# Weight products and averages moved to banks without other users, loads behind the first slot, the last two images drained apart (four-layer attention and mixer, one core)

## What is computed

```python
x = attention(x, L0)   # q, k of 16 channels, v of 128; gamma * softmax(q k^T) v + x
x = mixer(x, L1)       # 2-D Hartley transform, two block-diagonal layers with relu, shrink, back, + x
x = attention(x, L2)   # as layer 0
x = gn_attention(x, L3)  # group norm (32 groups), q, k, v of 128, softmax(q k^T / sqrt(128)) v wo + bo, + x
```

## Time and profile before

| what | us |
|---|---|
| median of the timed runs | 118.61 |
| the profiled execution, its own time | 117.25 |
| its span | 115.5 |
| PE busy | 102.2 (89%) |
| DVE, ACT, POOL busy | 69.5, 64.9, 56.3 |
| granted TensorE clock, mean | 0.992 |

### The profile page before, as it was taken

How to read it: one execution, slowest core, us unless ns; L and a number is a source line. 1 busy time by engine, 2 the same in 40 slices (tenths; PEclk the granted TensorE clock), 3 DMA queues, 4 the chain that set the end, 5 groups by cost and what they waited for, 6 DMA issues and landing times.

```text
span 115.5 us, 2858 instructions
## 1 busy us (share of the span) xinstructions
PE 102.2 (89%) x1004; PEld 86.9 (75%) x1004; DVE 69.5 (60%) x278; ACT 64.9 (56%) x186; POOL 56.3 (49%) x109
## 2 busy tenths in 40 slices
PE   5688799989997799999998699995999999999670
PEld 5267698989875688888887588974989797998540
DVE  0126567695977267777461869687586765466511
ACT  5028385756554166663647686755756554777520
POOL 0100390000576538888403364669987979844400
PEclk9999999999999999999999999999999999999996
DMA  2999400000000000000000000000000011101121
GB/s 83 215 271 414 178 0 0 6 3 0 3 6 0 0 0 0 6 0 0 0 6 0 3 9 0 0 0 0 6 0 0 0 45 45 48 25 49 48 68 45
DMA packets 3182, 4.57 MB, mean 40 GB/s; under 512 B 480, under 2 KB 2400, under 8 KB 3168
## 3 DMA queue, kind: packets, MB, share of 16 engines
q1 hardware_dynamic: 2160, 2.61, 7.3%
q10 hardware_dynamic: 1008, 1.78, 4.5%
HBM read 3.34 MB, written 1.05 MB: 38 GB/s over the span
## 4 chain that ended last, share of the span: by engine, by line
PE 74%; DMA 6%; ACT 6%; DVE 5%; POOL 3%; issue 3%; SPq 1%; DVEq 0%
PE banks L703 11%; PE banks L677 8%; PE banks L697 7%; PE banks L602 6%; PE banks L638 6%; DMA xt_in<-in_x_t 6%; PE banks L755 4%; PE banks L628 4%; PE banks L772 4%; PE banks L586 4%; PE banks L654 3%; PE banks L613 3%; PE banks L796 3%; ACT probs_t L893 3%; PE banks L734 2%
## 5 line engine op out<-in xcount | busy, mean ns | idle before, releaser
L504 POOL TENSOR_SCALAR hidden<-first,ident_columns 64x260 f32<-64x260 f32 x16 | 19.6, 1228 | 19.0 <-DVE first L1116 18.3
L885 ACT ACTIVATE probs<-negated,lowest 128x256 f32<-128x256 f32 x48 | 23.9, 500 | 7.5 <-DVE negated L1035 6.4
L452 POOL TENSOR_TENSOR probs<-probs,inverse 128x256 f32<-128x256 f32 x32 | 19.1, 612 | 15.8 <-DVE inverse L1049 15.4
L893 ACT ACTIVATE probs_t<-banks 128x512 f32<-128x512 f32 x24 | 14.3, 595 | 12.8 <-PE banks L677 12.7
L703 PE MATMUL banks<-probs_t,v 128*128 128x256 f32 x64 | 17.6, 397 | 1.6 <-ACT probs_t L893 1.6
L677 PE MATMUL banks<-ident_columns,probs 128*128 128x128 f32 x96 | 14.8, 275 | 1.4 <-issue 1.0
L1035 DVE TENSOR_SCALAR_CACHE_REDUCE negated<-banks 128x256 f32<-128x256 f32 x32 | 12.2, 416 | 2.7 <-PE banks L654 2.7
L703 PEld LDWEIGHTS banks<-probs_t,v 128*128 128x128 f32 x64 | 11.1, 190 | 3.5 <-ACT probs_t L893 2.3
L677 PEld LDWEIGHTS banks<-ident_columns,probs 128*128 128x128 f32 x96 | 11.1, 141 | 3.1 <-issue 1.5
L1049 DVE RECIPROCAL inverse<-total 128x1 f32<-128x1 f32 x48 | 7.2, 158 | 9.5 <-ACT probs L885 8.0
L1041 DVE TENSOR_SCALAR_CACHE_REDUCE negated<-banks,v 128x256 f32<-128x256 f32 x16 | 7.1, 480 | 5.1 <-PE banks L638 4.9
(11 more groups left out here) (109 smaller groups left out, 198.7 us busy)
## 6 DMA issues: line engine op xcount, KB each, us to landing
out<-stream SPq DMA_DIRECT2D x7, 128.0 KB, 1.9
rows<-in_x_rows ACTq DMA_DIRECT2D x1, 768.0 KB, 10.4
xt_in<-in_x_t SPq DMA_DIRECT2D x1, 512.0 KB, 8.5
constants<-in_constants SPq DMA_DIRECT2D x1, 450.0 KB, 10.1
layer<-in_layer ACTq DMA_DIRECT2D x1, 256.5 KB, 8.6
xt_in<-in_x_t SPq DMA_DIRECT2D x2, 128.0 KB, 4.1
rows<-in_x_rows ACTq DMA_DIRECT2D x1, 256.0 KB, 4.9
xt_in<-in_x_t SPq DMA_DIRECT2D x1, 256.0 KB, 6.8
```

Source lines behind the costliest of these rows:

```text
L452: pool.tensor_tensor(probs[:, half(job), tile, :], probs[:, half(job), tile, :], inverse[:, at, tile:tile + 1].to_broadcast([TILE, TOKENS] ...
L504: pool.tensor_scalar(halves(hidden[HC:C, half(job), side]), strided(first[own, half(job)], SUMS, -SUMS, SUMS), column["b1n"][own], 0.0, AL ...
L885: nc.scalar.activation(probs[:, half(job), tile, :], negated[:, half(job), tile, :], ACT.Exp, bias=lowest[:, half(job), tile:tile + 1], sc ...
L893: nc.scalar.activation(flat(probs_t[:, half(job)]), probs_t_bank, ACT.Copy).then_inc(probs_t_ready, 1)
```

## The change

No matmul is added or taken away. What moves:

- **Banks.** Weight products go to bank 2 (`prepared_strip`), two in a slot: mixer0 and mixer1 in slot 5, mixer2 and mixer3 in slot 7, weights3 and values3 in slot 19, bias3 in slot 21. `project_pair` and the first `forward_tokens` wait (`strip_taken`) until DVE has taken them. Averages go to banks 3 and 6 (means) and 2 and 7 (variances), each with the waits that this needs. The mixer's second product uses banks 0 and 1 in turn, g of image 0 bank 7. Bank 5 is left to the turned probabilities, which no longer wait for any of these.
- **Order.** In the slots of PE the energies of a pair come ahead of `forward_tokens`, and in slots 10 and 11 the second product ahead of `mix_values`. POOL normalizes first in its slot. 
- **Loads.** ACT issues x in rows and values after its part of slot 0, layer3 after slot 3.
- **End.** One drain slot is left for ACT and POOL, none for PE and DVE. The energies of the last image are made in its own slot. The last image but one gets its own banks and its probabilities are copied by DVE; the last one is scaled by DVE, and turned, copied, mixed, added and stored in two halves.

PE, slot 19: before, first product of the new layer's second pair to the next mix.

The diff, cut to its core:

```diff
-DRAIN = 3
+SLOTS = len(JOBS) + 1
+LAST = JOBS[-1]
...
-PREPARED = {3: "weights3", 4: "values3", 5: "mixer0", 6: "mixer1", 7: "mixer2", 8: "mixer3",
-            9: "bias3"}
+PREPARED = {5: ["mixer0", "mixer1"], 7: ["mixer2", "mixer3"], 19: ["weights3", "values3"],
+            21: ["bias3"]}
...
+        def prepared_strip(k):
+            return banks[:, 2, k * TOKENS:k * TOKENS + C + 3]
+        def mean_bank(pair):
+            return banks[:, 3 if pair < 2 else 6, 0:PAIR]
+        def variance_bank(pair):
+            return banks[:, 2 if pair == 0 else 7, 0:PAIR]
+        def g_bank(job):
+            return banks[:, 7 if job.image == 0 else 4, 0:TOKENS]
+        def y_bank(job):
+            return banks[:, half(job), 0:TOKENS]
...
+                if ahead is not None and ahead.layer == NORMED:
+                    normalize(ahead)
                 if spread_pair is not None:
                     channel_spreads(spread_pair)
                 if scale_pair is not None:
                     norm_scales(scale_pair)
-                if ahead is not None and ahead.layer == NORMED:
-                    normalize(ahead)
-                if scales(weighed):
+                if scales(weighed) and weighed != LAST:
                     scale_probs(weighed)
...
+            def project_pair(job, now):
+                if prepared_until(now):
+                    pe.wait_ge(strip_taken, prepared_until(now))
...
-                if job == Job(MIXER + 1, 0):
-                    pe.wait_ge(y_ready, BATCH)
-                elif job == Job(0, BATCH - 1):
-                    pe.wait_ge(y_ready, 1)
-                elif nth(job) > 1:
+                if nth(job) > 1:
                     pe.wait_ge(probs_t_ready, nth(job) - 1)
-                if sides_until(now):
-                    pe.wait_ge(side_taken, sides_until(now))
...
+            def transpose_last(tile):
+                if tile > 0:
+                    pe.wait_ge(probs_t_ready, nth(LAST) - 2)
+                pe.wait_ge(last_scaled, tile + 1)
...
+            def mix_last(tile):
+                pe.wait_ge(last_turned_ready, tile + 1)
...
                 if i == 0:
                     pe.wait_ge(mixer_ready, 6)
-                    pe.wait_ge(probs_t_ready, BATCH - 1)
-                    pe.wait_ge(side_taken, len(PREPARED))
+                if i < 2:
+                    pe.wait_ge(negated_ready, BATCH * TILES)
                 else:
-                    pe.wait_ge(probs_t_ready, BATCH)
-                    pe.wait_ge(y_ready, i)
+                    pe.wait_ge(y_ready, i - 1)
...
                 if i < 2:
                     pe.wait_ge(negated_ready, BATCH * TILES)
+                    pe.wait_ge(g_ready, 1)
...
             def group_variances(pair):
                 pe.wait_ge(spread_ready, pair + 1)
+                if pair == 0:
+                    pe.wait_ge(u_ready, 2 * BATCH)
+                else:
+                    pe.wait_ge(negated_ready, 2 * BATCH * TILES)
+                    pe.wait_ge(group_var_ready, pair)
...
-                if sides_until(now) > sides_until(now - 1) and by_age(now - 1, 3, 2):
-                    pe.wait_ge(probs_t_ready, nth(by_age(now - 1, 3, 2)))
...
+                    pe.wait_ge(u_ready, nth(this))
+                    for k, name in enumerate(PREPARED[now]):
+                        prepare(name, k)
+                if mixes(back2) and by_age(now, 4, 3):
+                    second_product(back2)
                 if by_age(now, 4, 3):
                     mix_values(by_age(now, 4, 3))
                 if mixes(back3):
                     backward_channels(back3)
-                if mixes(back2):
+                if mixes(back2) and not by_age(now, 4, 3):
                     second_product(back2)
...
+                if this == LAST:
+                    energies(this)
...
+            transpose_next_to_last()
+            mix_values(JOBS[-3])
+            mix_next_to_last()
+            for tile in range(TILES):
+                transpose_last(tile)
+            for tile in range(TILES):
+                mix_last(tile)
...
-            load_x(act, 0)
-            act.dma_start(values[:, :], values_d).then_inc(values_loaded, 16)
-            act.dma_start(layer3[:, :], layer3_d).then_inc(layer3_loaded, 16)
-            load_x(act, 1)
...
+                if now == 0:
+                    load_x(act, 0)
+                    act.dma_start(values[:, :], values_d).then_inc(values_loaded, 16)
+                    load_x(act, 1)
+                if now == 3:
+                    act.dma_start(layer3[:, :], layer3_d).then_inc(layer3_loaded, 16)
...
+            copy_next_to_last()
+            for tile in range(TILES):
+                invert_total(LAST, tile)
+                scale_last(tile)
+            add_residual(JOBS[-3])
+            add_next_to_last_residual()
+            for tile in range(TILES):
+                add_last_residual(tile)
```

More of the change, by code:

```diff
@@ L172, with prepared_until @@
            "gamma0", "gamma2", "bq0", "bk0", "bq2", "bk2"]
-def sides_until(slot):
-    made = [now for now in PREPARED]
-    for pair in range(BATCH // PAIR):
-        last = (NORMED - 1) * BATCH + pair * PAIR + PAIR - 1
-        made += [last + MEANS_AT, last + MEANS_AT + 1]
-    return sum(now <= slot for now in made)
+def prepared_until(slot):
+    return sum(len(names) for now, names in PREPARED.items() if now <= slot)
 def build(nc, x_rows_d, x_t_d, ident_columns_d, constants_d, plain_d, values0_d, values_d,
```

171 lines of the change are left out of this document (121 added, 50 removed).

## The result

| | before | after |
|---|---|---|
| median of the runs beside each other | 118.53 us (6 runs) | 109.97 us (6 runs) |
| their range | 117.37 to 119.95 | 109.82 to 110.37, one 113.76 |
| profiled execution, own time | 117.25 | 110.37 |
| its span | 115.5 | 108.6 |

The ratio is 0.931, 95% interval 0.926 to 0.936. The forecast was 112.1 us, the range 110.4 to 115.4: the time lies 0.4 us under its low end. Ratios leave out executions that lie more than 1.5% over the fastest of their kernel; medians here are over all of them.

The account below looks back on a forecast made before the run. PE, busy 102.2 of 115.5 us, was taken to bound the kernel, leaving gaps between its matmuls to shorten. Terms summed to -6.5: 110.75 profiled, 112.1 us with the timed runs' 1.36 offset; range 110.4 to 115.4.

Parts of the forecast that it names:

- step E: Slots 24 and 25: first normalized image sooner, but group_variances waits for spreads and a negation; -0.2 us, bias3 counted apart.
- A: Start to the first mix: weight products and waits gone, x sooner, less ACT's issues; -2.1 us.
- The 1.05 for ACT's issues: At the start: ACT's load issues delay its exponents and next copy, a cost of 1.05 us, between 0 and 2.36.
- The 0.7 for earlier x: At the start: the first two pieces of x land sooner with fewer loads beside them, a gain of 0.7 us.
- B: Slots 4 to 7: PE's wait in slot 7 for DVE to empty bank 5 goes, with its restart; -0.6 us.
- C: Slots 8 to 11, hand-over from layer 0 to the mixer: idle and restarts of 3.36 us fall to 1.2; -2.2 us.
- D: Slots 19 and 20: weights3 and values3 return, project_pair waits for DVE's takes; +0.6 us, between 0 and 1.25.
- F: Layer 3: projections no longer wait for POOL, about 0.43 us instead of 0.70; -0.5 us.
- G: The end: last image finished in halves, 2.8 us instead of 4.4 from exponents to residual; -1.5 us, between -0.7 and -2.
- Rival 1: At the start: the loads don't land sooner, constants still at 14.25; 114.0 us, chance 0.17.
- Rival 2: The removed waits come back elsewhere as DVE and ACT chains decide; 115.2 us, chance 0.18.
- Rival 3: ACT is held by its own load issues, so every exponent waits; slower, 120.3 us, chance 0.03.

Follow-up runs that it names:

- e11: Changed kernel with its four later loads issued by SyncE instead of ScalarE, behind the same events: 109.65 us.
- e10: Changed kernel with the mixer's second product back in bank 5 and its third back in bank 4: 112.88 us.
- e8: Changed kernel with projection ahead of energies in slot 18 and prepared products taken before the values are moved in slot 19: 109.48 us, ratio 0.923.
- e4: Changed kernel with the end as before (three draining slots, general code for the last images): 111.51 us.
- e1: The kernel before, unchanged, timed again: 118.79 us, ratio 1.001.
- e13: Changed kernel with one warm-up product instead of three: 111.3 us.
- e6: Kernel before with the later loads moved behind the first slot and five warm-up products instead of three: 117.35 us, ratio 0.992.
- e2: Kernel before with only the loads of x in rows, values and layer3 moved behind the first slot: 119.99 us.
- e12: Kernel before with five warm-up products instead of three, loads all up front: 118.25 us, ratio 1.001.
- e5: Kernel before with four warm-up products instead of three, loads all up front: 117.94 us.
- e9: The changed kernel, unchanged, timed again: 110.07 us, ratio 0.927.
- e14: Changed kernel with the two orders of e8 and the SyncE loads of e11 together: median 111.53 us, best 108.53.
- e15: e14 with four warm-up products instead of three: 109.25 us, ratio 0.919.
- e7: Changed kernel with four warm-up products instead of three: 110.32 us.

## Why the prediction was nearly right, and where it failed

**The mechanism and the sum.** Against its own profiled execution the forecast was 110.75 us; measured 110.37. Only step E has the wrong sign, by 0.4 us.

- **A** gained 2.57, not 2.1, and for other reasons. The 1.05 for ACT's issues was nothing (e11, and what the exponents waited for): a time of issue on ACT's queue was added to a chain that hangs on VectorE. I had the idle 1.32 us in hand and subtracted it as if the issues came behind each other with the moves; they run beside the moves. By the Trainium skill ("DMA: Bandwidth & Descriptors", section "Issuing engines are not separate DMA queues") initiating is usually small relative to the DMA; the rows of 0.33 to 0.59 us, two beside the moves and one inside the wait, agree beside 4.7 to 6.2 us to landing, and the total by that rule, 111.1, was nearer. The 0.7 for earlier x did not come either: the pieces landed 0.5 us sooner, and the first projection ran at half speed and took 0.86 us more, so that the values start where they did (6.64 and 6.67). That a cost of 1.05 us which did not come and a gain of 0.7 which did not come partly cancel is luck. The constants landed at 9.2, so POOL's diagonals were ready at 12.3, and mixer0 was asked for at 15.26: covered, as forecast.
- **B and C** were forecast as -3.3 with bias3 and came as -2.95. B was -0.7 for -0.6; C was -1.7 for -2.2. The waits that C left were named: in slot 9 the copy holds the mix for 0.24 us, the second product of image 0 waits 0.29. What was mis-sized is the restart. Its 0.28 us is the difference between a mix of 1.17 and one of 0.89. But a mix right behind the second product takes 1.09 without any wait:

```profile
33.03 0.59 PE banks L829 x8
33.62 1.09 PE banks L726 x8
```

  Two such mixes stand in this stretch, so about 0.4 us (an estimate from these rows) of the restarts' price stayed. e10 shows that the banks are what removed the rest.
- **D** +1.12 for +0.6. The wait for the strip was foreseen (0.61 here); the 0.37 us and restart of layer 2's first energies behind y of the last image were not. The diff puts `y_ready` in front of them, since y now lies in the banks of the energies. e8 removes both: 1.05.
- **E** -0.10, forecast +0.29 with bias3, which came back at 0.22 us to the next step and not at its 0.49 from behind a wait; so its move was a gain of 0.27 and not 0 in all. `group_variances` waits 0.6 us as said, but for POOL's spreads, not for the negation.
- **F** and **G** -0.77 and -1.63 for -0.5 and -1.5; e4 gives G back at 1.54. In G the total is better than its terms: from the last exponents to the last residual it takes 3.3 us, not 2.8, and the stretch behind the last residual, which was to stay, fell from 2.6 to 2.2. That they cancel is luck.

**The step that failed** is the last one: "The three timed runs have a median 1.36 above the profiled one; I carry the difference over: 118.61 - 6.5 = **112.1 us**". That difference is no constant of the chip. The traces and warm-up runs put it at the start of the kernel before, and the change took it away: the changed kernel's median lies 0.40 *below* its profiled execution. Two things make it:

1. How long TensorE stays at half speed. It differs by execution with the same code and the same idle time ahead of it: no slow real product (first profile), 40 and some more (e1, whose first mix is 1.04 us later). Less warm-up makes it long (e13: 96 products, 3.2 us at the first mix), more makes it short (e6 against e2: -2.6 us by the median).
2. Loads of later stages in flight with the first images (e12 against e6: +0.9 us and the wider spread; the waits of 1.33 and 0.53 us in e5). This one rests on medians and is less well shown.

Read back: e6 is the kernel before with neither, and its median of 117.35 us is close to the 117.25 of the profiled execution. In part that is chance: e6 waits 0.98 us for layer3, and the first profile 0.44 and 0.56 us for the second and third piece of x. From 117.35 the -6.5 gives 110.85, and the measured steps' -6.9 gives 110.45. The last 0.5 us down to 109.97 is again the start: e9's profiled execution, of the same kernel, took 109.93 us with its first mix at 12.42, 0.43 sooner, of which 0.23 by an earlier first piece of x and 0.20 by a projection of 1.74 us instead of 1.94. The range should have reached down to 117.25 - 6.5 less the two low ends, about 109.1.

The Trainium skill ("TensorE: Matmul & The Clock Gate", section "Part 1: The HAM clock gate (the "warmup" mystery)") says that the number of slow matmuls at the start differs from run to run of one kernel, which e1 shows beside the first profile (40 and none). It also puts the cost of it at under 1% of a typical kernel's time; here the medians of e2 and e6 differ by 2.6 of 120 us, 2.2%, and this measurement decides.

**Open.** What decides that one execution starts slow and the next one not, with the same kernel, the runs do not show: e14 with a gap of only 0.24 us in its best execution has four of 110.5 us and more. That timelines exist only for the profiled executions is the reason; for the others the cause is inferred from how warm-up changes their spread. Three executions of the kernel before took 123.84 to 124.34 us (one in e1, two beside e5 to e8), and nothing here explains them. Not tried: the pairs of weight products without the other parts, and POOL's new order (E, F) alone.

**The rivals.** Rival 1 (loads land no sooner) fell for the constants, 5.6 us instead of 10.1, and for the wait for images 2-3, which is gone. The first two pieces of x gained only 0.5 us, less than the 0.7 and far from the near doubling that the rival's text considered. Rival 2 (waits come back elsewhere) holds for D alone. Rival 3 (ACT held by its issues) fell: the 768 KB load was issued in 0.59 us, and no run here shows an issue that waits for room.

## What to carry to other kernels

Before you turn a gain into a time, look at how the runs of the kernel before scatter, and find where in the kernel the profiled execution differs from its median: an offset that sits at the start belongs to the start, and a change that touches it changes it. Compare the durations of one repeated instruction at the start and later; if they differ nearly twofold, try giving TensorE work up to the moment at which its first inputs land, and judge by the spread of the runs, since the best execution gets no better by it. It paid in e6 and e15, and not in e7. When banks are freed and an order is changed together, ask of each moved product which wait it now carries past the work behind it (e10).

## What the runs showed of the hardware

- At the start TensorE runs its matmuls nearly twice as long (32 in 1.94 us for 1.08, 8 in 2.08 for 1.16), for none to 96 of the first real ones (first profile, e13), with a granted clock printed as 1.00 all the while. The two levels are 1.2 and 2.4 GHz; here only the durations tell them apart. In e5 and e6 the change already shows inside the warm-up, whose matmuls go from 634 to 380 ns.
- DMA issues on ScalarE's queue (0.33 and 0.56 us) run beside its activations.
- With ACT's 1.47 MB issued later, 450 KB land in 5.6 to 6.4 us instead of 10.1 to 11.4. The first two pieces of 128 KB land in 3.2 to 4.1 instead of 4.0 to 4.4: little of a first load's time is the others' doing.
- What a matmul group costs to the next step depends on what stands ahead of it, without any wait: in the changed kernel's chain the eight matmuls of a mix take 0.89 us behind weight products (at 15.71), and 1.09 behind a projection (at 12.85) or the mixer's second product (at 33.62). A single weight product behind the projection took 0.42 and behind another one 0.22, so most of that 0.20 is passed on, and not saved, where a mix takes its place. Why is not shown.
